# Attention layer, one core: one key bank of each row maximum read as a difference, with a relu on ScalarE

## The chip, the cores and the metric

The kernel runs on one core of one Trainium2 chip. The metric is the device time of one execution in microseconds, the median of several runs. The trace is of one profiled execution of its own.

## The reference

The input is x of shape (2, 4096, 256). It is layer-normalised to xn. The output is x + attention(xn) + experts(xn). The experts are eight small gated networks with routing weights. The attention has 16 heads of 16 columns, in two batches, so 32 heads in all:

```python
q, k, v = (xn @ W.T + b for each)            # reshaped to 16 heads of 16 columns
scores = einsum('bqhd,bkhd->bhqk', q * 16 ** -0.5, k)      # 4096 x 4096 per head
probs = softmax(scores)
out = einsum('bhqk,bkhd->bqhd', probs, v) @ Wo.T + bo
```

The kernel subtracts each row's maximum before the exponentials, so the maximum over the 4096 scores of a row is needed first.

## The kernel before

There are four phases. A setup phase splits the weights into a high and a low part. The token phase (16 groups of 512 tokens, g) computes the norm, the routing, the experts, and q, k and v. For q and k ScalarE writes the high part (L425) and VectorE the low part (L575), and SP stores both to `parts_d`. The attention phase follows, and an output phase ends the kernel.

The attention goes over 64 half heads (`s`): for each of 32 heads, first the queries 0 to 2047 and then 2048 to 4095. Two things run side by side for a half head.

- Scores of the half head `s` itself, transposed: keys on partitions, 512 queries as columns. `score` (L857) fills one of three banks `st`, ScalarE's exp (L951) reads it into a ring of 16 slots `pr`, and `times_v` (L865) multiplies by V, with a column of ones for the denominator, into `pv`. Four products for four groups of queries run in four column groups of the array. `values` issues them for the key block two behind.
- Maxima of the half head `s + 1`: `max_bank` (L844) computes 128 queries against 512 keys into one of four banks `sc`. A tile is 128 queries and eight such banks (`BANKS`). VectorE reduces the banks to six numbers per query (`MAXIMA`): banks 0 and 1 in one instruction, 2, 3, then 4 and 5 in one, 6, 7 (L971). The maxima run two tiles ahead (`AHEAD`).

The rows of q and k stand twice in SBUF: partitions 0 to 49 serve the scores, partitions 64 to 111 the maxima. So a score and a maxima matmul can run at the same time in two row groups of the array. In the loop over `r` (16 tiles per half head) TensorE issues for each of eight `i` one score and one maxima matmul; after i = 2 the products of one key block in whole width (512 columns), after i = 5 and i = 7 those of the next block in two halves of 256 columns.

Each engine has its own order of instructions, written out by hand, and semaphores between them: a score waits until the exp of three scores before has been read (`st_read`), a maxima matmul until the bank of four before has been reduced (`sc_read`), an exp waits for its score (`st_full`), a maximum for its banks (`sc_full`). When all maxima of a half head are there, VectorE turns them into two rows of the query operand in four small instructions (L976, L980, L984, L991). Once per half head ScalarE copies the sums `pv` to `oT` (`sums_kept`, L940), after the exps of key block 1 of the next half head; the products of key block 2 wait for it (`sums_ready`). Once per head VectorE inverts the denominators (L997).

The maxima of the first half head, and two tiles of the second, run before any score: first banks 0 to 3 of all 16 tiles, then banks 4 to 7 (`first_order`). In the last half head no maxima are left; the scores then use seven banks and alternate between the two row groups.

SP loads the rows of the next head from `parts_d` in 12 transfers (`head_rows`), spread over the head before; `qk_loaded` counts them.

Of the kernel before, what the change touches and what calls it, by code (L numbers as in the profile page):

```python
# [11 lines left out]
P = 128  # L12
# [34 lines left out]
TINY = 1e-8  # L47
DMA = 16
# [41 lines left out]

def first_head(nc, c, parts):

    for part_n in parts:
        w, half = ((0, 0), (1, 0), (1, 1), (0, 1))[part_n]
        for grp in range(2):
            for term in range(3):
                head_rows(nc, c, w, 0, 0, grp, term, half * QH, QH).then_inc(c.first_in[part_n], DMA)
# [116 lines left out]
def token_phase(nc, a, c):  # L214
    with ExitStack() as ctx:
# [3 lines left out]
        xn = sb("xn", [P, TPG, D], F32)  # L219
        xT = [[sb(f"xT{i}{hl}", [P, KC, GT], F32R) for hl in range(2)] for i in range(2)]  # L220
# [42 lines left out]
        vchain = sem("vector_chain")  # L263
        passed = sem("passed")
# [14 lines left out]
        def _(sp):  # L279
# [44 lines left out]
            sp.wait_ge(last_base_stored, DMA)  # L324
            for i in range(2):
# [74 lines left out]
        def _(act):  # L400
# [9 lines left out]
            def misc_unit(g, par, n):  # L410
# [12 lines left out]
                bias = c.bqs if kind == "q" else c.bk  # L423
                act.wait_ge(parts_stored[u % 2], (g * (SPLITS // 2) + u // 2 + 1) * DMA)
# [9 lines left out]
            def body(g, par, last, more):  # L434
                for e in range(E):
# [17 lines left out]
        def _(pool):  # L453
            def base_start(g, par):
# [4 lines left out]
                ins.then_inc(base_init, 1)  # L459

# [4 lines left out]
            def body(g, par, last, more):  # L465
                for e in range(E):
# [4 lines left out]
                    if e == 0 and not last:  # L471
                        base_start(g + 1, 1 - par)

# [5 lines left out]
        def _(dve):  # L479
# [78 lines left out]
            def misc_unit(g, par, n):  # L558
# [62 lines left out]
def attention_phase(nc, a, c):  # L621
# [3 lines left out]
    with ExitStack() as ctx:  # L625
# [4 lines left out]
        oT = sb("oT", [P, GT], F32)  # L630
        mx = [sb(f"mx{i}", [P, QT, MAXIMA], F32) for i in range(2)]
# [16 lines left out]
        sc_read = sem("sc_read")  # L648
        max_chain = sem("max_chain")
# [21 lines left out]
        QK_LOADS = 2 * 3 * 2  # L671
        V_LOADS = 4
# [26 lines left out]

        def reductions(g):  # L700

            return 3 * (g // RINGB) + (1, 1, 2, 3)[g % RINGB]
# [18 lines left out]
        def first_order(g):  # L721

            if g >= QT * BANKS:
                return divmod(g % (QT * BANKS), BANKS)
            half, rest = divmod(g, QT * RINGB)
            return rest // RINGB, half * RINGB + rest % RINGB

        @block.sync
        def _(sp):
            def load(n, par, piece):  # L730

                w, rest = divmod(QK_LOADS - 1 - piece, QK_LOADS // 2)
                grp, term = divmod(rest, 3)
                head_rows(nc, c, w, par, n, grp, term, 0, S).then_inc(qk_loaded, DMA)
# [103 lines left out]
        def _(pe):  # L838
            def max_bank(g, t, b, par, hf, grp):

                r0, q0 = 64 * grp, hf * QH + t * P
                if g >= RINGB:
                    pe.wait_ge(sc_read, reductions(g - RINGB))
# [27 lines left out]
            for g in range((QT + AHEAD) * BANKS):  # L871
                for part_n in WHEN_IN.get(g, ()):
                    pe.wait_ge(c.first_in[part_n], 2 * 3 * DMA)
                t, b = first_order(g)
                max_bank(g, t, b, 0, g // (QT * BANKS), g % 2)
            pe.wait_ge(c.ones_in, RING * 2 * DMA)

            def body(h0, heads, at):
                first, last = at == 0, at + heads == HEADS
                for q in range(2 * heads):  # L880
# [16 lines left out]
                    if here == SUPERS - 1:  # L897
                        for kb in range(KB):
                            for j in range(QSUB):
                                score(s, QSUB * kb + j, par, hf, here, j % 2)  # L900
                            values(kb, 0, GT)
                        continue
                    for r in range(KB // 2):
                        t = r + AHEAD
                        to = q + 1 + t // QT
                        if hf == 0 and t == QT and not (last and q // 2 == heads - 1):
                            pe.wait_ge(qk_loaded, (n + 1) * QK_LOADS * DMA)
                        for i in range(BANKS):
# [23 lines left out]
        def _(act):  # L932
# [32 lines left out]
        def _(dve):  # L965
            def maximum(g, t, i, par):

                c, col = divmod(i, 3)
                first, n = ((0, 2), (2, 1), (3, 1))[col]
                dve.wait_ge(sc_full, g + RINGB * c + first + n)  # L970
                nc.vector.reduce_max(mx[par][:, t, i:i + 1], sc_bank(first, n), AX.X).then_inc(sc_read, 1)  # L971
# [27 lines left out]
            for half in range(2):  # L999
                for t in range(QT):  # L1000
                    for i in range(3 * half, 3 * half + 3):
                        maximum((half * QT + t) * RINGB - half * RINGB, t, i, 0)
# [4 lines left out]
            for t in range(AHEAD):  # L1007
                for i in range(MAXIMA):
                    maximum((QT + t) * BANKS, t, i, 1)

            def body(h0, heads, at):
                first, last = at == 0, at + heads == HEADS
                for q in range(2 * heads):
                    s = 2 * h0 + q
                    for r in range(KB // 2):
                        t = r + AHEAD
                        to = s + 1 + t // QT
                        for i in range(MAXIMA):
                            if to < SUPERS:
                                maximum(((s + 1) * QT + t) * BANKS, t % QT, i, to % 2)  # L1020
# [124 lines left out]
def layer(nc, x, Wq, bq, Wk, bk, Wv, bv, Wo, bo, Wg, Wu, Wd, Wr, temperature, out):  # L1145
# [8 lines left out]
    c.base_d = nc.dram_tensor("base_d", (TOK, D), F32, kind="Internal").ap()  # L1154
    c.v_d = nc.dram_tensor("v_d", (TOK, D), F32, kind="Internal").ap()
# [40 lines left out]
```

## Time and profile before

| | |
|---|---|
| median of 3 runs | 6275.22 us (6273.61 to 6275.73) |
| profiled execution | 6268.36 us |
| its span, first to last instruction | 6266.6 us |
| TensorE busy | 6156.2 us (98%) |
| VectorE busy | 5532.0 us (88%) |
| ScalarE busy | 4840.4 us (77%) |
| GpSimd busy | 512.8 us (8%) |

The token phase ends at about 1300 us; the maxima run from 1316.0 to 6116.4 us. A busy share is an average over the stages. An instruction's duration runs from its start to the end of its writes; neighbours on one engine overlap, so the distance between two starts can be less than the duration.

### The profile page before, as it was taken

The numbers are of one execution on the slowest core, as the hardware profiler recorded it, in microseconds if no ns is written. First come the engines' busy times: TensorE is split into PE (matmuls) and PEld (weight loads), VectorE is DVE, ScalarE is ACT, GpSimd is POOL, SyncE is SP. The second block draws the span as 40 slices with busy tenths as digits, with TensorE's granted clock in tenths as the row PEclk, the third lists the DMA queues.
The fourth block names the chain that finished last, engine by engine and source line by source line (L and its number), as shares of the span: only waits on it lengthen the run. The fifth ranks groups of instructions, "written<-read, shape, count | busy, mean of one in ns | idle before, by whom it ended". The sixth has DMA issues, their size and how long they took to land. (4 is left out here: it accounts for less than half of the span.)

```text
span 6266.6 us, 120405 instructions
## 1 busy us (share of the span) xinstructions
PE 6156.2 (98%) x48392; PEld 3140.4 (50%) x48392; DVE 5532.0 (88%) x8291; ACT 4840.4 (77%) x9069; POOL 512.8 (8%) x535
## 2 busy tenths in 40 slices
PE   6999999989999999999999999999999999999998
PEld 5888888854444444444444444444444444444444
DVE  5555555579999999999999999999999999999993
ACT  3444333318898888888988888988889898988886
POOL 2333322210000000000000000000000000000000
PEclk9999999969999999999999999999999999999999
DMA  3111111111111121111111111111111111111113
GB/s 100 48 48 48 48 48 48 41 28 27 34 34 34 35 36 32 30 30 30 31 31 31 30 31 30 31 31 30 30 30 30 35 34 34 34 34 35 34 50 129
DMA packets 243304, 244.68 MB, mean 39 GB/s; under 512 B 159472, under 2 KB 204272, under 8 KB 236400
## 3 DMA queue, kind: packets, MB, share of 16 engines
q1 hardware_dynamic: 231720, 206.04, 15.0%
q0 software_dynamic: 11024, 30.94, 2.1%
q8 instruction: 379, 6.21, 0.4%
q14 instruction: 181, 1.48, 0.1%
HBM read 159.26 MB, written 76.58 MB: 38 GB/s over the span
## 5 line engine op out<-in xcount | busy, mean ns | idle before, releaser
L971 DVE TENSOR_REDUCE mx<-sc 128x1 f32<-128x512 f32 (+1 forms) x6144 | 4785.1, 856 | 9.4 <-PE sc L844 8.9
L951 ACT ACTIVATE pr<-st 128x512 f32<-128x512 f32 x8120 | 4268.0, 603 | 479.1 <-PE st L857 475.1
L844 PE MATMUL sc<-experts 48*128 48x512 f32 x8192 | 2824.6, 446 | 21.4 <-DVE mx L971 13.8
L857 PE MATMUL st<-experts 50*128 50x512 f32 x8120 | 2694.7, 431 | 0.1
L865 PE MATMUL pv<-pr,vst 128*32 128x256 f32 (+1 forms) x24440 | 2397.0, 464 | 2.0 <-ACT pr L951 0.9
L857 PEld LDWEIGHTS st<-experts 50*128 50x128 f32 x8120 | 1306.6, 184 | 1827.2 <-ACT pr L951 1654.6
L844 PEld LDWEIGHTS sc<-experts 48*128 48x128 f32 x8192 | 1328.5, 186 | 92.6 <-DVE mx L971 75.1
L865 PEld LDWEIGHTS pv<-pr,vst 128*32 128x32 f32 x24440 | 481.7, 108 | 955.3 <-issue 907.8
L438 ACT ACTIVATE gated<-gate 128x512 f32<-128x512 f32 x256 | 152.0, 597 | 567.3 <-PE up L75 567.0
L606 DVE TENSOR_TENSOR hraw<-gated,up 128x512 f32<-128x512 f32 x256 | 174.5, 686 | 416.4 <-ACT gated L438 404.2
L75 PE MATMUL down<-experts,hid 128*128 128x256 f32 x3072 | 390.2, 283 | 15.1 <-POOL hid L469 15.1
L469 POOL TENSOR_TENSOR hid<-hraw,hid 128x512 fp32r<-128x512 f32 x256 | 325.6, 1293 | 890.9 <-ACT hid L441 890.9
L75 PEld LDWEIGHTS down<-experts,hid 128*128 128x128 f32 x3072 | 384.2, 191 | 27.0 <-POOL hid L469 18.3
L75 PE MATMUL gate<-xT,experts 128*128 128x512 f32 x1536 | 392.9, 391 | 0.0
L75 PE MATMUL up<-xT,experts 128*128 128x512 f32 x1536 | 389.8, 389 | 0.0
L75 PEld LDWEIGHTS up<-xT,experts 128*128 128x128 f32 x1536 | 288.4, 188 | 60.2
L822 POOL DMA_DIRECT2D den<-den_d x32 | 17.3, 540 | 3626.9 <-DMA den_d<-oT 3626.9
L75 PEld LDWEIGHTS gate<-xT,experts 128*128 128x128 f32 x1536 | 283.2, 188 | 55.1
L587 DVE SCALAR_TENSOR_TENSOR base<-down,wts,base 128x256 f32<-128x256 f32 x512 | 222.6, 478 | 74.8 <-PE down L75 74.3
L441 ACT ACTIVATE hid<-hraw 128x512 fp32r<-128x512 f32 x256 | 160.5, 629 | 47.7 <-DVE hraw L606 47.7
L75 PE MATMUL misc<-xT,wT 128*128 128x512 f32 x384 | 95.7, 399 | 6.4 <-DVE part L575 6.4
L824 POOL DMA_DIRECT2D rden_d<-rden x32 | 17.2, 538 | 879.6 <-DVE rden L997 879.6
(105 smaller groups left out, 1280.9 us busy)
## 6 DMA issues: line engine op xcount, KB each, us to landing
experts<-parts_d SPq DMA_DIRECT2D x372, 256.0 KB, 4.3
parts_d<-part SPq DMA_DIRECT2D x64, 512.0 KB, 2.8
x_in<-in_L_attn_hidden_states SPq DMA_DIRECT2D x16, 512.0 KB, 4.6
v_d<-v_sb SPq DMA_DIRECT2D x32, 256.0 KB, 2.1
vst<-v_d SPq DMA_DIRECT2D x128, 64.0 KB, 2.2
sums_d<-oT SPq DMA_DIRECT2D x256, 32.0 KB
whole<-sums_d POOLq DMA_DIRECT2D x32, 256.0 KB, 3.0
recs<-rden_d POOLq DMA_DIRECT2D x32, 256.0 KB, 5.5
```

The lines of the kernel that those rows point to most:

```text
L75: last = nc.tensor.matmul(out, lhs[k][a], rhs[k][b], start=(n == 0), stop=(n == len(terms) - 1))
L438: nc.scalar.activation(gated[half][:, :], gate[half][:, :], ACT.Silu).then_inc(silu_done, 1)
L441: nc.scalar.activation(hid[e % 2][0][:, half, :], hraw[half][:, :], ACT.Identity).then_inc(hh_ready, 1)
L469: nc.gpsimd.tensor_tensor(hid[e % 2][1][:, half, :], hraw[half][:, :], hid[e % 2][0][:, half, :], ALU.subtract).then_inc(hl_ready, 1)
L587: ins = nc.vector.scalar_tensor_tensor(out=base[par][:, t, :], in0=down[hf][:, j, :], scalar=wts[par][:, t, e:e + 1], in1=base[par][:, t, ...
L606: nc.vector.tensor_tensor(hraw[half][:, :], gated[half][:, :], up[half][:, :], ALU.mult).then_inc(hid_ready, 1)
L822: nc.gpsimd.dma_start(den[:, :], c.den_d[bass.ds(n, 1), :].rearrange("o (p f) -> (o p) f", p=P)).then_inc(den_in, DMA)
L844: nc.tensor.matmul(sc_bank(g % RINGB), qr[par][r0:r0 + TERMS, q0:q0 + P], kr[par][r0:r0 + TERMS, b * GT:(b + 1) * GT], start=True, stop=Tr ...
L857: nc.tensor.matmul(score_bank(at, x), kr[par][r0:r0 + ROWSM, kb * P:(kb + 1) * P], qr[par][r0:r0 + ROWSM, q0:q0 + GT], start=True, stop=Tr ...
L865: last = nc.tensor.matmul(pv[VC * j:VC * (j + 1), c0:c1], vst[par][:, kb, :], pr[:, (QSUB * kb + j) % PRING, c0:c1], start=(kb == 0 and c0 ...
L951: nc.scalar.activation(pr[:, (QSUB * kb + j) % PRING, :], score_bank(2 * at + q, x), ACT.Exp).then_inc(st_read, 1)
L971: nc.vector.reduce_max(mx[par][:, t, i:i + 1], sc_bank(first, n), AX.X).then_inc(sc_read, 1)
```

## The change

The maximum of the last two key banks is rewritten. For a query, with s6 and s7 its scores against one key of group 6 and the key of group 7 at the same place, max(s6, s7) = s6 + relu(s7 - s6), and s7 - s6 is one matmul against the difference of the keys, k7 - k6. The token phase makes these key differences (`kd`, for two groups per batch), splits them into a high and a low part and stores them to `kd_d`. In the partitions that serve the maxima, the last 512 columns of k hold them in place of the last keys (`difference_rows`). Bank 6 of a tile is then filled from the difference, bank 7 from the keys of group 6. ScalarE reads bank 6 with a relu into `ahead` in SBUF (`above`, after the exp of x % 8 == 6), and VectorE does one `tensor_tensor_reduce` of bank 7 and `ahead`, add and then maximum. VectorE reduces a tile in six instructions as before, now banks 0 and 1 together, 2, 3, 4, 5, and 7 with `ahead`. The maxima matmul that refills bank 6 waits for the relu, not for VectorE.

The products with V are issued at other places of the tile, the first head's tiles follow the same scheme, and a head's rows come in 15 transfers. In the last four key blocks of the last half head the scores use only row group 0, since the other group no longer holds these keys.

```diff
+def difference_rows(nc, c, par, n, term):
+    r0 = 64 + HD * term
+    return nc.sync.dma_start(kept_rows(c, par)[1][r0:r0 + HD, S - GT:S].bitcast(F32), c.kd_d[ORDER[1][term], n * HD:(n + 1) * HD, :])
...
+                if kind == "k" and g % GPB == GPB - 2:
+                    if g >= GPB:
+                        act.wait_ge(kd_stored, g // GPB * KC * DMA)
+                    nc.scalar.activation(kd[:, 1, i, :].bitcast(F32), bank[:, :], ACT.Identity, bias=bias[:, i:i + 1]).then_inc(k_kept, 1)
...
+                        if e == E - 1 and (g + 1) % GPB == GPB - 1:
+                            for i in range(KC):
+                                act.wait_ge(k_apart, (g + 1) // GPB * KC + i + 1)
+                                nc.scalar.activation(kd[:, 0, i, :], kd[:, 1, i, :].bitcast(F32), ACT.Identity).then_inc(kd_high, 1)
...
+            def store_difference(b):
+                for i in range(KC):
+                    pool.wait_ge(kd_high, b * KC + i + 1)
+                    nc.gpsimd.tensor_tensor(kd[:, 1, i, :], kd[:, 1, i, :].bitcast(F32), kd[:, 0, i, :], ALU.subtract).then_inc(kd_low, 1)
+                for i in range(KC):
+                    pool.wait_ge(kd_low, b * KC + i + 1)
+                    pool.dma_start(c.kd_d[:, b * D + i * P:b * D + (i + 1) * P, :].rearrange("r p t -> p r t"),
+                                   kd[:, :, i, :].bitcast(F32)).then_inc(kd_stored, DMA)
...
+                    if kind == "k" and g % GPB == GPB - 1:
+                        dve.wait_ge(k_kept, g // GPB * KC + i + 1)
+                        nc.vector.scalar_tensor_tensor(out=kd[:, 1, i, :].bitcast(F32), in0=misc[(par * len(MISC) + n) % 2][:, :], scalar=bias[:, i:i + 1],
+                                                       in1=kd[:, 1, i, :].bitcast(F32), op0=ALU.add, op1=ALU.subtract).then_inc(k_apart, 1)
...
+        DIFFERENCE = BANKS - 2
+        KEYS_APART = tuple(range(DIFFERENCE)) + (BANKS - 1, DIFFERENCE)
...
-                if g >= RINGB:
-                    pe.wait_ge(sc_read, reductions(g - RINGB))
+                before = g - RINGB
+                if before >= 0:
+                    if placed(before)[1] == DIFFERENCE:
+                        pe.wait_ge(d_read, placed(before)[0] + 1)
+                    else:
+                        pe.wait_ge(sc_read, reductions(before))
+                b = KEYS_APART[b]
...
-                            if i == 2:
-                                values(2 * r, 0, GT)
-                            if i == 5:
-                                values(2 * r + 1, 0, GT // 2)
-                            if i == 7:
-                                values(2 * r + 1, GT // 2, GT)
+                            if i == 1:
+                                values(2 * r, 0, GT // 2)
+                            if i == 3:
+                                values(2 * r, GT // 2, GT)
+                            if i == 6:
+                                values(2 * r + 1, 0, GT)
...
+            def above(g):
+                if g >= SUPERS * QT * BANKS:
+                    return
+                tile = placed(g)[0]
+                act.wait_ge(sc_full, g + 1)
+                if tile >= 2:
+                    act.wait_ge(sc_read, reductions(last_bank(tile - 2)))
+                nc.scalar.activation(ahead[:, tile % 2, :], sc_bank(g % RINGB), ACT.Relu).then_inc(d_read, 1)
+            for t in range(QT + AHEAD):
+                above(last_bank(t) - 1)
...
+                            if x % BANKS == DIFFERENCE:
+                                above(((s + 1) * QT + kb // 2 + AHEAD) * BANKS + DIFFERENCE)
...
+            def maximum(g, tile, i):
+                first, n = ((0, 2), (2, 1), (3, 1), (4, 1), (5, 1), (7, 1))[i]
+                column = mx[tile // QT % 2][:, tile % QT, i:i + 1]
+                dve.wait_ge(sc_full, g + first + n)
+                if first < DIFFERENCE:
+                    nc.vector.reduce_max(column, sc_bank(first % RINGB, n), AX.X).then_inc(sc_read, 1)
+                    return
+                dve.wait_ge(d_read, tile + 1)
+                nc.vector.tensor_tensor_reduce(out=summed[:, :], in0=sc_bank(first % RINGB), in1=ahead[:, tile % 2, :], scale=1.0, scalar=LOWEST,
+                                               op0=ALU.add, op1=ALU.max, accum_out=column).then_inc(sc_read, 1)
```

## Rows read from the trace of the kernel before

**Rows 1.** The page, its first part: span, and busy us by engine.

```profile
span 6266.6 us, 120405 instructions
PE 6156.2 (98%) x48392; PEld 3140.4 (50%) x48392; DVE 5532.0 (88%) x8291; ACT 4840.4 (77%) x9069; POOL 512.8 (8%) x535
```

**Rows 2.** Busy time by stage: token, first maxima, steady stretch; columns in the first row.

```profile
core 0: us, PE busy (x) PEld busy (x) DVE busy (x) ACT busy (x) POOL busy (x), PEclk, DMA share, GB/s
200.00:1200.00 1000.00, 987.76 (x5742) 875.50 (x5741) 540.36 (x1427) 397.70 (x612) 299.91 (x258) 1.00 0.14 47
1316.00:1400.00 84.00, 70.17 (x145) 30.47 (x145) 83.86 (x111) 0.57 (x1) 0.00 (x0) 0.50 0.16 23
2500.00:3500.00 1000.00, 999.96 (x8538) 410.31 (x8534) 1000.00 (x1344) 898.61 (x1721) 25.58 (x38) 1.00 0.16 29
```

**Rows 3.** Groups by form, 2500 to 3500 us: busy, mean ns, idle before.

```profile
L951 ACT ACTIVATE pr<-st 128x512 f32<-128x512 f32 x1708 | 894.7, 598 | 101.4 <-PE st L857 100.6
```

**Rows 4.** Timeline of one tile: start us, length us, engine, line, instruction.

```profile
3000.50 1.57 ACT L951 ACTIVATE pr<-st 128x512 f32<-128x512 f32 x3 [0.21 <-PE st L857]
...
3000.80 1.06 PE L865 MATMUL pv<-pr,vst 128*32 128x512 f32 x8
...
3001.79 0.49 PE L857 MATMUL st<-experts 50*128 50x512 f32 x1
...
3002.10 0.18 PEld L844 LDWEIGHTS sc<-experts 48*128 48x128 f32 x1
...
3002.13 0.46 PE L844 MATMUL sc<-experts 48*128 48x512 f32 x1
...
3002.32 2.62 ACT L951 ACTIVATE pr<-st 128x512 f32<-128x512 f32 x5 [0.25 <-PE st L857]
...
3002.75 0.64 PE L865 MATMUL pv<-pr,vst 128*32 128x256 f32 x8
...
3003.32 0.50 PE L857 MATMUL st<-experts 50*128 50x512 f32 x1
...
3003.66 0.39 PE L857 MATMUL st<-experts 50*128 50x512 f32 x1
...
3004.55 0.50 PE L857 MATMUL st<-experts 50*128 50x512 f32 x1
```

**Rows 5.** Timeline of VectorE alone in the same tile, four of its instructions.

```profile
3000.84 1.21 DVE L971 TENSOR_REDUCE mx<-sc 128x1 f32<-128x1024 f32 x1
...
3002.57 0.67 DVE L971 TENSOR_REDUCE mx<-sc 128x1 f32<-128x512 f32 x1
3003.16 1.21 DVE L971 TENSOR_REDUCE mx<-sc 128x1 f32<-128x1024 f32 x1
3004.30 0.67 DVE L971 TENSOR_REDUCE mx<-sc 128x1 f32<-128x512 f32 x1
```

**Rows 6.** Timeline where a half head's sums are copied out.

```profile
3056.44 0.60 ACT L940 ACTIVATE oT<-pv 128x512 f32<-128x512 f32 x1
...
3056.91 1.60 ACT L951 ACTIVATE pr<-st 128x512 f32<-128x512 f32 x3
...
3057.14 1.06 PE L865 MATMUL pv<-pr,vst 128*32 128x512 f32 x8
```

**Rows 7.** Groups by form, 2500 to 3500 us: VectorE's small operations.

```profile
L976 DVE TENSOR_REDUCE nm<-mx 128x16 f32<-128x96 f32 x14 | 3.3, 237 | 0.0
...
L991 DVE STREAM_TRANSPOSE turned<-nmp 128x32 f32<-128x32 f32 x14 | 2.7, 196 | 0.0
L984 DVE TENSOR_TENSOR nmp<-nm,nmp 128x16 fp32r<-128x16 f32 x14 | 2.2, 159 | 0.0
L980 DVE CAST nmp<-nm 128x16 fp32r<-128x16 f32 x14 | 2.2, 158 | 0.0
L997 DVE RECIPROCAL rden<-den 128x32 f32<-128x32 f32 x6 | 2.0, 336 | 0.0
```

**Rows 8.** Chain of work that ended last: start us, length us, two adds.

```profile
6234.10 1.30 DVE o_base L1136 x2
```

More of the change, by code:

```diff
@@ L47 @@
 TINY = 1e-8
+LOWEST = -3.4028234663852886e38
 DMA = 16
@@ L96, in first_head @@
             for term in range(3):
-                head_rows(nc, c, w, 0, 0, grp, term, half * QH, QH).then_inc(c.first_in[part_n], DMA)
+                split = w and half and grp
+                head_rows(nc, c, w, 0, 0, grp, term, half * QH, QH - GT if split else QH).then_inc(c.first_in[part_n], DMA)
+                if split:
+                    difference_rows(nc, c, 0, 0, term).then_inc(c.first_in[part_n], DMA)
 def setup_phase(nc, a, c):
@@ L263, in token_phase @@
         vchain = sem("vector_chain")
+        k_kept = sem("second_last_keys_kept")
+        k_apart = sem("keys_subtracted")
+        kd_high = sem("difference_high_ready")
+        kd_low = sem("difference_low_ready")
+        kd_stored = sem("difference_stored")
         passed = sem("passed")
@@ L324, in _ @@
             sp.wait_ge(last_base_stored, DMA)
+            sp.wait_ge(kd_stored, B * KC * DMA)
             for i in range(2):
@@ L472, in body @@
                         base_start(g + 1, 1 - par)
+                    if e == E - 1 and (g + 1) % GPB == GPB - 1 and not last:
+                        store_difference((g + 1) // GPB)
             in_groups(before, body)
@@ L630, in attention_phase @@
         oT = sb("oT", [P, GT], F32)
+        ahead = sb("ahead", [P, 2, GT], F32)
+        summed = sb("summed", [P, GT], F32)
         mx = [sb(f"mx{i}", [P, QT, MAXIMA], F32) for i in range(2)]
@@ L648, in attention_phase @@
         sc_read = sem("sc_read")
+        d_read = sem("difference_read")
         max_chain = sem("max_chain")
@@ L671, in attention_phase @@
         QK_LOADS = 2 * 3 * 2
+        QK_MOVES = QK_LOADS + 3
         V_LOADS = 4
@@ L698, in sc_bank, with placed, last_bank @@
             return sc[:, i * GT:(i + n) * GT]
-        def reductions(g):
-            return 3 * (g // RINGB) + (1, 1, 2, 3)[g % RINGB]
+        COUNT = (1, 1, 2, 3, 4, 5, 5, 6)
+        def placed(g):
+            if g >= QT * BANKS:
+                return divmod(g, BANKS)
+            half, rest = divmod(g, QT * RINGB)
+            return rest // RINGB, half * RINGB + rest % RINGB
+        def reductions(g):
+            tile, i = placed(g)
+            if g >= QT * BANKS:
+                return MAXIMA * tile + COUNT[i]
+            return COUNT[3] * tile + COUNT[i] + (COUNT[3] * (QT - 1) if i >= RINGB else 0)
+        def last_bank(tile):
+            return QT * RINGB + RINGB * tile + RINGB - 1 if tile < QT else tile * BANKS + BANKS - 1
+        DIFFERENCE = BANKS - 2
+        KEYS_APART = tuple(range(DIFFERENCE)) + (BANKS - 1, DIFFERENCE)
         WHEN_IN = {0: (0, 1), QT * RINGB: (2,), QT * BANKS: (3,)}
@@ L719, in rows_of @@
             return dram[g * GT:(g + 1) * GT, :].rearrange("(t p) d -> p t d", p=P)
[L721 to L726, printed above, removed]
         @block.sync
@@ L733, in load @@
                 grp, term = divmod(rest, 3)
-                head_rows(nc, c, w, par, n, grp, term, 0, S).then_inc(qk_loaded, DMA)
+                split = w and grp
+                head_rows(nc, c, w, par, n, grp, term, 0, S - GT if split else S).then_inc(qk_loaded, DMA)
+                if split:
+                    difference_rows(nc, c, par, n, term).then_inc(qk_loaded, DMA)
             def load_v(n, par, piece):
@@ L872, in _ @@
                 for part_n in WHEN_IN.get(g, ()):
-                    pe.wait_ge(c.first_in[part_n], 2 * 3 * DMA)
-                t, b = first_order(g)
-                max_bank(g, t, b, 0, g // (QT * BANKS), g % 2)
+                    pe.wait_ge(c.first_in[part_n], (9 if part_n == 2 else 6) * DMA)
+                t, b = placed(g)
+                max_bank(g, t % QT, b, 0, g // (QT * BANKS), g % 2 if g < QT * RINGB else 1 - g % 2)
             pe.wait_ge(c.ones_in, RING * 2 * DMA)
@@ L899, in body @@
                             for j in range(QSUB):
-                                score(s, QSUB * kb + j, par, hf, here, j % 2)
+                                score(s, QSUB * kb + j, par, hf, here, j % 2 if kb < KB - GT // P else 0)
                             values(kb, 0, GT)
@@ L906, in body @@
                         if hf == 0 and t == QT and not (last and q // 2 == heads - 1):
-                            pe.wait_ge(qk_loaded, (n + 1) * QK_LOADS * DMA)
+                            pe.wait_ge(qk_loaded, (n + 1) * QK_MOVES * DMA)
                         for i in range(BANKS):
@@ L1001, in _ @@
                     for i in range(3 * half, 3 * half + 3):
-                        maximum((half * QT + t) * RINGB - half * RINGB, t, i, 0)
+                        maximum((half * QT + t) * RINGB - half * RINGB, t, i)
             negated(0, 0)
@@ L1008, in _ @@
                 for i in range(MAXIMA):
-                    maximum((QT + t) * BANKS, t, i, 1)
+                    maximum((QT + t) * BANKS, QT + t, i)
             def body(h0, heads, at):
@@ L1019, in body @@
                             if to < SUPERS:
-                                maximum(((s + 1) * QT + t) * BANKS, t % QT, i, to % 2)
+                                maximum(((s + 1) * QT + t) * BANKS, (s + 1) * QT + t, i)
                             if t == QT and s + 1 < SUPERS:
```

7 lines of the change are left out of this document (2 added, 5 removed).

## Prediction

> **What bounds the kernel now.** I read the page for the time of each engine, the windows for the stages, the groups of the steady stretch by form, and then the timeline of one tile. The profiled run took 6268.36 us for a span of 6266.6 [rows 1]; the median shown is 6275.22, so 7 us are added to my sum at the end. Four fifths of the span is the attention. There VectorE has no idle time (1000.00 of 1000 us), TensorE is busy for 999.96 and ScalarE for 898.6 [rows 2]. A busy TensorE says little, so I lay out a tile (128 queries against 4096 keys).
>
> VectorE: single-bank maxima start 0.60 us apart and a double takes 1.13 until the next start [rows 5]. Four singles and two doubles make 4 x 0.598 + 2 x 1.131 = 4.65 us. The trace gives eight exps in 8 x 1000 / 1708 = 4.68 us per tile [rows 3]. The rest of 0.03 are the small operations of the row maxima: 0.16, 0.08, 0.08 and 0.12 us per half head (their durations less the 0.08 by which neighbours overlap) and one reciprocal of 0.26 per head [rows 7], about 0.57 us per 16 tiles. So VectorE sets the pace.
>
> TensorE, if nobody held it: a group of two pairs (score and maxima matmul side by side) takes 0.66 from its first start to the products with V, one of three 0.89, each further pair 0.235; the products take 0.99 in whole width and 0.57 in half [rows 4] (3000.80 to 3001.79; 3002.75 to 3003.32). Sum 0.89 + 0.89 + 0.66 + 0.99 + 0.57 + 0.57 = 4.58. That is only 0.08 under the pace. ScalarE: three exps in 1.57 us, the first 0.60 long, so 0.49 each in a chain; eight are 3.9.
>
> **The change, part by part.** (1) VectorE loses one bank of eight: before, the second double and two singles (1.13 + 1.20) took banks 4 to 7; now two singles (1.20) and one add-and-maximum. The trace has no such operation. The nearest rows are an add of a PSUM and an SBUF operand, two in 1.30, 0.61 each in a row [rows 8], and small operations that cost 0.08 in a row [rows 7]. From below it is 0.60 (the maximum as an operation of one pass); from above 0.80, if the reduced value is fetched in an operation of its own that costs a full 0.20, the duration of the transpose of 32 columns [rows 7]. I take 0.60 + 0.07 = 0.67, near the small ones. VectorE's own work is then 1.13 + 4 x 0.60 + 0.67 = 4.19 per tile: no longer a bound by itself, and not what decides.
>
> The Trainium skill, "VectorE: DVE Perf Modes", section "Two Vector instructions with no wait between them", says that an operation that also writes out its accumulator is two instructions, the main one and an accumulator read. No row here shows it; it has no figure for the second, and it speaks for the upper half of the bounds.
>
> (2) ScalarE gets a relu per tile between exps 6 and 7, and the add-and-maximum waits for it. The same form in the same chain (oT, between exps) costs 0.47 to the next start [rows 6], so 0.49: nine are 4.41, plus 0.49 of oT per 16 tiles, 4.44 per tile. Not a bound by sum, but ScalarE now has hardly any slack, and the score ring has three banks. What counts is the loop of waits. From rows 4: a score's result comes 0.49 after the group starts; exp begins 0.04 later (3001.79 + 0.49 to 3002.32) and lasts 0.60. A bank whose reader ends is filled 0.55 later (double ended 3000.84 + 1.21 = 3002.05 [rows 5], load 3002.10, matmul ends 3002.59). Products with V start 0.07 before the last result ends (3003.66 + 0.39 against 3004.55 - 0.57).
>
> *Loop A*, one tile: score 4 is first of its group: 0.49 + 0.04 + 0.60 = 1.13 until exp 4 ends; exps 5, 6, relu, exps 7 and 0: 5 x 0.49 = 2.45; score 3 needs exp 0's bank: 0.55; then -0.07 + 0.57 of products until score 4 starts: 0.50. Sum 4.63. Without the relu it is 4.14, which is why it does not show now.
>
> *Loop B*, two tiles: exp 4 ends 1.13, relu ends 3 x 0.49 = 1.47 later; add-and-maximum 0.04 + 0.67 + 0.08; the next tile's double 1.13, then bank 2's maximum 0.60, whose release lets bank 6 be filled, 0.55; -0.07 + 0.99 of whole-width products; then TensorE alone to score 4: 0.89 + 0.57 + 0.66 + 0.57 = 2.69. Sum 9.28, half of it 4.64. So both loops leave 4.64 where 4.654 was: the bank saved yields 0.014 per tile, 0.2 us per half head.
>
> (3) The products with V are moved: half width after pair 1, half after pair 3, whole after pair 6. The floor stays 4.58. But the first ones of a half head's third block wait until ScalarE has copied the accumulator out (oT). Now that copy ends at 3057.04 and the products start at 3057.14 instead of about 3057.06: met almost exactly [rows 6]. After the change, counted from score 4 of the tile before: exps end at 1.13, e7 behind the relu 4 x 0.49 later, the copy 0.49 later: 3.58, plus 0.09 until products start: 3.67. TensorE would be there at 0.89 + 0.99 + 0.89 = 2.78, or 2.9 with loop B's delay. So this wait, with exps 0 to 2 queued behind the copy and all of TensorE behind the products, costs 0.8 us per half head. VectorE's small operations (0.16 + 0.08 + 0.08 + 0.12 = 0.44, and 0.13 for half a reciprocal) lie in loop B. All could cost 1.4; the loops absorb a little of one another, I take 1.3.
>
> Sum per half head (16 tiles): before 16 x 4.654 + 0.57 = 75.03; after 16 x 4.64 + 1.3 = 75.54. That is +0.5, times 63 half heads with maxima running beside them: +32 us.
>
> (4) The first head: 18 tiles run before ScalarE has exps, and VectorE is busy 83.86 of 84 us although TensorE's clock is at 0.50, its 1.2 GHz level [rows 2]. Banks 4 to 7 cost 2.33 now and 1.20 + 0.67 = 1.87 then: -0.46 x 18 = -8 us. The relu runs on an idle engine.
>
> (5) Token stage: for two key groups of 16, two more ScalarE copies of 0.6 us, two VectorE passes of 0.7 and, once a batch, two ScalarE copies, two GpSimd subtractions of about 1.3 and two stores. TensorE is busy 988 of 1000 us there, the others 540, 398 and 300 [rows 2]: hidden, +1. If that cover failed: under 4 us per batch. SP issues 15 loads per head instead of 12, same bytes, at 0.16 DMA share [rows 2], with the wait for them far off: 0.
>
> (6) The last half head: in its last four key blocks the scores lose the alternation of row groups. Four in one group take 1.13 and the products 0.99 against ScalarE's 4 x 0.49 = 1.96: at most 4 x 0.16. +0.5.
>
> Total 32 - 8 + 1.5 = +25: 6268.4 + 25 = 6293 for the profiled execution, 6300 beside the median of 6275.2.
>
> **Rivals.** A change under 0.2% (12.5 us) can't be told from none.
> *TensorE becomes the bound (faster).* The loops rest on latencies of a few hundredths. If a filled bank follows its release by 0.45 and not by 0.55, both loops fall to or under the floor of 4.58, and only the wait for oT stays: 16 x 4.58 + 0.85 = 74.13, -0.9 x 63 - 8 = -65: 6210. For it speaks that VectorE has half a microsecond per tile to give; against it that 0.55 is read from a real wait. It wins once the loops are under 4.62. Chance 0.22.
> *Gain and loss cancel.* The add-and-maximum at 0.60 and the loops at A's 4.63: 16 x 4.63 + 1.1 = 75.2, +9 - 9: 6275. Chance 0.15 of within 0.2% with its neighbours.
> *The add-and-maximum is dear.* At 0.80 loop B is 4.70: 16 x 4.70 + 1.3 = 76.5, +1.5 x 63 = +93, first head -6: 6362. At 1.0, 4.80: 6460. Chance 0.15.
> *ScalarE's chain is slower with the relu.* If each of the five links of loop A cost 0.03 more (0.11 more is the upper bound, an exp's whole 0.60 without overlap), the loop would be 4.63 + 0.15 = 4.78: 16 x 4.78 + 1.0 = 77.5, +2.5 x 63 - 8 = +150: 6425. Rows of this form speak against it: 0.49 in the chain of three [rows 4], 0.47 between starts around oT [rows 6]. Chance 0.03.
> The Trainium skill, "ScalarE: Activation LUTs", section "What ACT_TABLE_LOAD costs", gives an ACTIVATE with immediate scale and bias 186 ns + 0.833 N, less 93 ns overlap back to back: an estimate of 0.52 us for 512 columns. That is about this rival's link. The trace has 0.49, and by the trace I go.
> *My forecast*, loops at 4.63 to 4.67: chance 0.45.
>
> **Numbers.** 6300, itself 6285 to 6330. The range takes in most of the faster case and the dear operation: 6215 to 6370. Faster 0.23, same 0.16, slower 0.61.
>
> **What would show it.** VectorE idle for about 0.4 us per tile, put down to ScalarE's relu; ScalarE at 94 to 95% busy; the relu in chains of 0.49; half heads of 75.5 us; a TensorE stall of 0.8 us on oT once per half head; first maxima stage 8 us shorter; next start after an add-and-maximum 0.67 later. The forecast is wrong if VectorE idles and half heads are under 74.8 (latencies shorter than laid out, or the copy of oT hidden), or if that operation takes over 0.75.

## The result, and the profile after

The changed kernel takes 6362.53 us, median of 4 runs (6361.88 to 6364.21), against 6275.4 for the kernel before. The ratio is 1.0141, with a 95% interval from 1.0127 to 1.0155: 87 us slower. The forecast was 6300 and slower: 25 us more, where 87 were measured.

The page of the changed kernel, its first part:

```profile
span 6360.1 us, 124618 instructions
...
PE 6205.0 (98%) x48392; PEld 3169.6 (50%) x48392; DVE 5104.6 (80%) x9319; ACT 5214.5 (82%) x10101; POOL 520.0 (8%) x543
```

Beside [rows 1]: VectorE (DVE) has lost 427 us of work, ScalarE (ACT) has gained 374, and the span has grown by 93.5. The stages tell where. The windows of the changed kernel; columns as in [rows 2]:

```profile
200.00:1200.00 1000.00, 987.77 (x5743) 875.47 (x5742) 543.36 (x1430) 401.09 (x618) 303.59 (x262) 1.00 0.14 48
1316.00:1400.00 84.00, 74.48 (x174) 34.25 (x176) 80.74 (x138) 17.59 (x30) 1.05 (x4) 0.50 0.19 24
2500.00:3500.00 1000.00, 990.53 (x8360) 407.31 (x8352) 891.19 (x1523) 954.75 (x1895) 27.48 (x41) 1.00 0.17 31
```

In the steady stretch VectorE now idles for 109 of 1000 us, and no other engine is full in its place: ScalarE 955, TensorE 991 instead of 999.96. If no engine is full, something else must set the pace; the forecast said that it would be a loop of waits.

The first start of the maxima and of the scores, from the list of instructions on the tiles `sc` and `st`; before, then after. The length of the first maxima stage is the distance between the two first starts:

```profile
L844 PE MATMUL sc<-experts x8192: 383/447/793, 1315.1 to 6115.2; 48*128 48x512 f32 x200
...
L857 PE MATMUL st<-experts x8120: 383/394/794, 1398.6 to 6185.7; 50*128 50x512 f32 x199
```
```profile
L908 PE MATMUL sc<-experts x8192: 383/491/794, 1316.6 to 6206.9; 48*128 48x512 f32 x200
...
L921 PE MATMUL st<-experts x8120: 383/394/792, 1392.1 to 6277.9; 50*128 50x512 f32 x199
```

The token stage ends 1.5 us later. The first maxima stage takes 75.5 us instead of 83.5: 8 less. For the half heads I use the copies of the sums, one per half head. Before, then after; min/median/max ns, first and last start:

```profile
L940 ACT ACTIVATE oT<-pv x64: 597/605/685, 1482.0 to 6190.3; 128x512 f32<-128x512 f32 x64
```
```profile
L1004 ACT ACTIVATE oT<-pv x64: 592/594/637, 1475.7 to 6281.8; 128x512 f32<-128x512 f32 x64
```

The copy before the last one starts at 6221.2 after the change and at 6129.6 before it: the last half head, without maxima, takes 60.6 and 60.7. The 62 others take (6281.8 - 1475.7 - 60.6) / 62 = 76.54 us each, where they took (6190.3 - 1482.0 - 60.7) / 62 = 74.96. That is +1.58 a half head, +98 us over 62. With +1.5, -8 and +2 in the tail it makes the 93.5 of the spans. So the whole loss is in the steady half heads. I call this number "half head" below.

The groups of the steady stretch, 2500 to 3500 us of the changed kernel, by form:

```profile
L1028 ACT ACTIVATE pr<-st 128x512 f32<-128x512 f32 x1673 | 871.4, 610 | 45.3 <-PE st L921 43.6
...
L1054 DVE CUSTOM_DVE_ANT_0 summed<-sc,ahead 128x512 f32<-128x512 f32 x210 | 145.2, 691 | 106.5 <-PE sc L908 90.7 <-ACT ahead L1014 15.1
L1014 ACT ACTIVATE ahead<-sc 128x512 f32<-128x512 f32 x209 | 129.2, 618 | 0.0
...
L1054 DVE DVE_READ_ACCUMULATOR2_ANT mx<- 128x1 f32 x209 | 17.3, 83 | 0.0
```

Nearly all of VectorE's idle time stands before the add-and-maximum: 106.5 of 109 us, for 210 of them. The accumulator read is an instruction of its own, of 83 ns. What it costs is in the timeline of one tile of the changed kernel:

```profile
3001.06 0.62 ACT L1014 ACTIVATE ahead<-sc 128x512 f32<-128x512 f32 x1
...
3001.54 2.59 ACT L1028 ACTIVATE pr<-st 128x512 f32<-128x512 f32 x5
...
3001.82 0.69 DVE L1054 CUSTOM_DVE_ANT_0 summed<-sc,ahead 128x512 f32<-128x512 f32 x1 [0.81 <-ACT ahead L1014]
...
3002.44 0.08 DVE L1054 DVE_READ_ACCUMULATOR2_ANT mx<- 128x1 f32 x1
3002.44 3.61 DVE L1051 TENSOR_REDUCE mx<-sc 128x1 f32<-128x1024 f32 x5
...
3003.71 0.49 PE L921 MATMUL st<-experts 50*128 50x512 f32 x1
...
3004.30 1.57 ACT L1028 ACTIVATE pr<-st 128x512 f32<-128x512 f32 x3 [0.17 <-PE st L921]
...
3005.75 0.62 ACT L1014 ACTIVATE ahead<-sc 128x512 f32<-128x512 f32 x1
```

The next maximum starts with the accumulator read, 0.62 after the add-and-maximum: the read is free. From relu to relu the tile takes 4.69 us, not 4.64. And here is the missing piece: score 4 starts at 3003.71 and ends at 3004.20; exp 4 starts at 3004.30. That is 0.10 later, and so it is in 205 of the 209 tiles of this stretch. The 0.04 of the forecast came from exp 3 [rows 4], which waits only for its score. Exp 4 is the first of a key block and waits also for a free slot of `pr`. That wait had long been met: the products that free the slot ran from 2999.92 to 3000.98. The trace before had this too, at exp 0, two rows that I did not use:

```profile
2999.90 0.50 PE L857 MATMUL st<-experts 50*128 50x512 f32 x1
...
3000.50 1.57 ACT L951 ACTIVATE pr<-st 128x512 f32<-128x512 f32 x3 [0.21 <-PE st L857]
```

The add-and-maximum too waits for two things (bank 7 and the relu): the relu ends at 3001.06 + 0.62 = 3001.68, it starts at 3001.82, 0.14 later. The profile books most of this wait (90.7 us) to bank 7's matmul and 15.1 us to the relu. But the start stands 0.14 behind the relu's end in 207 of the 209 tiles, and at changing distances behind the matmul, so it is the relu that releases it. With these two values loop A is 4.63 + 0.06 = 4.69, and loop B (9.28 - 0.05 + 0.06 + 0.10) / 2 = 4.69 or 4.70. Both are equal to the tile that the trace shows.

Once per half head the copy of the sums stops TensorE:

```profile
3006.75 0.60 ACT L1004 ACTIVATE oT<-pv 128x512 f32<-128x512 f32 x1
...
3007.40 0.64 PE L929 MATMUL pv<-pr,vst 128*32 128x256 f32 x8 [0.71 <-ACT oT L1004]
```

The copy ends at 3007.35 and the products start at 3007.40. The third score of their group had started at 3006.29. In the tile before, such products started 0.33 us behind the third score's start, so these could have started at 3006.62. The stall is 0.78 us.

### The profile page after: what moved, and what is told of

Its sections match the earlier page's. It is cut to its first block and busy times, and to the rows that moved or that the text cites. A ratio compares the mean times of both kernels' runs of the same rounds, so it can differ in the third digit from the quotient of the medians.

```text
span 6360.1 us, 124618 instructions
## 1 busy us (share of the span) xinstructions
PE 6205.0 (98%) x48392; PEld 3169.6 (50%) x48392; DVE 5104.6 (80%) x9319; ACT 5214.5 (82%) x10101; POOL 520.0 (8%) x543
## 5 line engine op out<-in xcount | busy, mean ns | idle before, releaser
L1051 DVE TENSOR_REDUCE mx<-sc 128x1 f32<-128x512 f32 (+1 forms) x5120 | 3719.2, 787 | 24.0 <-PE sc L908 24.0
L908 PE MATMUL sc<-experts 48*128 48x512 f32 x8192 | 2877.8, 451 | 17.4 <-PEq L225 9.4
L921 PEld LDWEIGHTS st<-experts 50*128 50x128 f32 x8120 | 1335.6, 184 | 1942.0 <-ACT pr L1028 1819.5
L908 PEld LDWEIGHTS sc<-experts 48*128 48x128 f32 x8192 | 1352.2, 186 | 73.8 <-DVE mx L1051 40.2
L1054 DVE CUSTOM_DVE_ANT_0 summed<-sc,ahead 128x512 f32<-128x512 f32 x1024 | 707.9, 691 | 510.3 <-PE sc L908 441.3
L1014 ACT ACTIVATE ahead<-sc 128x512 f32<-128x512 f32 x1024 | 632.8, 618 | 79.3 <-PE sc L908 79.3
L76 PE MATMUL down<-experts,hid 128*128 128x256 f32 x3072 | 390.1, 283 | 15.1 <-POOL hid L504 15.1
```

What stands on the lines that cost most here:

```text
L76: last = nc.tensor.matmul(out, lhs[k][a], rhs[k][b], start=(n == 0), stop=(n == len(terms) - 1))
L908: nc.tensor.matmul(sc_bank(g % RINGB), qr[par][r0:r0 + TERMS, q0:q0 + P], kr[par][r0:r0 + TERMS, b * GT:(b + 1) * GT], start=True, stop=Tr ...
L921: nc.tensor.matmul(score_bank(at, x), kr[par][r0:r0 + ROWSM, kb * P:(kb + 1) * P], qr[par][r0:r0 + ROWSM, q0:q0 + GT], start=True, stop=Tr ...
L1014: nc.scalar.activation(ahead[:, tile % 2, :], sc_bank(g % RINGB), ACT.Relu).then_inc(d_read, 1)
L1051: nc.vector.reduce_max(column, sc_bank(first % RINGB, n), AX.X).then_inc(sc_read, 1)
L1054: nc.vector.tensor_tensor_reduce(out=summed[:, :], in0=sc_bank(first % RINGB), in1=ahead[:, tile % 2, :], scale=1.0, scalar=LOWEST, op0=AL ...
```

## The experiments

All ran against the kernel before. The half heads are from the first and last start of the oT copies of each run, as above (last half head 60.6 to 61.1).

| run | median us | ratio (95% interval) | half head us |
|---|---|---|---|
| before | 6273 to 6275 | | 74.96 |
| after | 6362.53 | 1.0141 (1.0127 to 1.0155) | 76.54 |
| e1 wait off exp 4 | 6329.94 | 1.0089 (1.0074 to 1.0104) | 76.01 |
| e2 copy of sums earlier | 6341.67 | 1.0107 (1.0090 to 1.0124) | 76.20 |
| e3 no relu | 6236.14 | 0.9938 (0.9923 to 0.9953) | 74.50 |
| e4 before, products moved | 6312.83 | 1.0061 (1.0046 to 1.0076) | 75.58 |
| e5 relu that nobody waits for | 6267.39 | 0.9990 (0.9981 to 1.0000) | 75.02 |
| e6 e1 and e2 | 6306.51 | 1.0052 (1.0037 to 1.0067) | 75.63 |
| e7 products at the old places | 6647.18 | 1.0594 (1.0578 to 1.0610) | 81.02 |
| e8 relu after exp 2 | 6278.28 | 1.0007 (0.9998 to 1.0016) | 75.21 |
| e9 e8 with the double on banks 0, 1 | 6286.19 | 1.0022 (1.0014 to 1.0031) | 75.35 |
| e10 e8 with the wait off exp 0 | 6225.46 | 0.9924 (0.9910 to 0.9937) | 74.33 |

### e1: the slot wait moved off exp 4

```diff
-                        act.wait_ge(pv_done, s * KB + kb + 1)
+                        if 2 * at + q == SUPERS - 1:
+                            act.wait_ge(pv_done, s * KB + kb + 1)
+                        elif kb % 2 == 0:
+                            act.wait_ge(pv_done, s * KB + kb + 2)
```

> The changed kernel with one wait moved: the wait of exp for a free slot of pr (pv_done) stands ahead of exp 0 of each tile for both key blocks, no longer ahead of exp 4. Theory 1 (loop A sets the pace, and its missing 0.06 us is that exp 4, which waits for two things, starts 0.10 after its score and not 0.04): a tile falls from 4.70 to 4.64 or 4.65, a half head from 76.5 to 75.7, the time from 6362 to 6310 to 6325. Theory 2 (loop B, through the add-and-maximum, sets the pace by itself): its exp 4 link is shorter too, but half as much per tile: 76.1 per half head, 6335 to 6345. Theory 3 (ScalarE or a port is slower for another reason): no change, 6362.

It took 6329.94 us, 33 less than the changed kernel. Exp 4 now starts right behind its score (3104.25 + 0.50 to 3104.78), and the relus, one per tile, stand like this:

```profile
3104.25 0.50 PE L921 MATMUL st<-experts 50*128 50x512 f32 x1
```
```profile
3104.78 0.60 ACT L1031 ACTIVATE pr<-st 128x512 f32<-128x512 f32 x1
...
3101.52 0.62 ACT L1014 ACTIVATE ahead<-sc 128x512 f32<-128x512 f32 x1
...
3106.23 0.62 ACT L1014 ACTIVATE ahead<-sc 128x512 f32<-128x512 f32 x1
...
3110.86 0.62 ACT L1014 ACTIVATE ahead<-sc 128x512 f32<-128x512 f32 x1
```

These tiles alternate, 4.71 and 4.63. 4.63 is loop A without the 0.06. The pair takes 9.34, 4.67 a tile, which is what a loop over two tiles does: loop B is left, (9.28 - 0.05 + 0.10) / 2 = 4.665. Not every tile alternates: from 3012 to 3058 us they take 4.65 to 4.69, which is the same over two. The time lies between theories 1 and 2, and the half head, 76.01, next to the 76.1 of theory 2: the double wait costs what was said, and behind it the second loop stands 0.04 lower.

### e2: the copy of the sums before exp 7

```diff
-                        if kb == 1 and not (first and q == 0):
-                            sums_kept(s - 1)
...
+                            if kb == 1 and j == DIFFERENCE - QSUB and not (first and q == 0):
+                                sums_kept(s - 1)
```

> The changed kernel with the copy of the sums (oT) between the relu and exp 7 of the half head's first tile, one link earlier. Theory 1 (the products of key block 2 stand still 0.8 us per half head because the copy sits behind the relu and exp 7): the stall falls from 0.8 to 0.3, part of it comes back because exp 7 is 0.49 later; 0.3 to 0.4 us less per half head, 6338 to 6345. Theory 2 (the copy waits for the last products of the half head before, not for ScalarE's order): nothing changes, 6362.

It took 6341.67 us, 21 less; a half head lost 0.34. In the list of waits, 2500 to 3500 us, the products stood for 5.0 us on 7 copies in the changed kernel and for 1.5 in this one. The waits at the six other copies of the stretch are in a row of their own, without a releaser: 4.5 us and 1.6.

```profile
PE pv L929 <- ACT oT L1004: 5.0, 7, 0.7
PE pv L929 <- issue: 4.5, 6, 0.8
```
```profile
PE pv L929 <- issue: 1.6, 6, 0.3
PE pv L929 <- ACT oT L1004: 1.5, 7, 0.2
```

The stall comes from the place of the copy in ScalarE's order.

### e3: no relu

After the first 18 tiles this kernel leaves the relu out. The add-and-maximum reads a tile of zeros (`nothing`) instead, so the maximum leaves out the keys of group 7, and the matmul that refills bank 6 waits for nothing. The core of the edit:

```diff
-                            if x % BANKS == DIFFERENCE:
-                                above(((s + 1) * QT + kb // 2 + AHEAD) * BANKS + DIFFERENCE)
...
-                        pe.wait_ge(d_read, placed(before)[0] + 1)
+                        if placed(before)[0] < QT + AHEAD:
+                            pe.wait_ge(d_read, placed(before)[0] + 1)
...
-                dve.wait_ge(d_read, tile + 1)
+                dve.wait_ge(d_read, min(tile, QT + AHEAD - 1) + 1)
...
-                nc.vector.tensor_tensor_reduce(out=summed[:, :], in0=sc_bank(first % RINGB), in1=ahead[:, tile % 2, :], scale=1.0, scalar=LOWEST,
+                nc.vector.tensor_tensor_reduce(out=summed[:, :], in0=sc_bank(first % RINGB), in1=ahead[:, tile % 2, :] if tile < QT + AHEAD else nothing[:, :], scale=1.0, scalar=LOWEST,
```

> The changed kernel without the relu after the first 18 tiles: the add-and-maximum reads a constant tile of zeros, so bank 6 counts for nothing in the maximum. Theory 1 (the relu's link in ScalarE's chain sets the pace): loop A falls to 4.20, and TensorE alone is left with 4.58 a tile; half head 74.4, the time 6225 to 6235, under the kernel before. Theory 2 (the add-and-maximum or its accumulator read costs the time): half head stays near 76.5, 6350 to 6362. Theory 3 (TensorE's own work has grown by the moved products): half head 75 or more, 6270 and over.

It took 6236.14 us, 126 less than the changed kernel and less than the kernel before. The add-and-maximum, its accumulator read and the moved products are all still there, and so is the stall on the copy. Most tiles take 4.58 to 4.60. The half head is 74.50 = 16 x 4.58 + 1.2: TensorE's floor and what stops it. So it is the relu and what waits for it that cost the time, and VectorE's relief was real.

### e4: the kernel before with the products moved

```diff
-                            if i == 2:
-                                values(2 * r, 0, GT)
-                            if i == 5:
-                                values(2 * r + 1, 0, GT // 2)
-                            if i == 7:
-                                values(2 * r + 1, GT // 2, GT)
+                            if i == 1:
+                                values(2 * r, 0, GT // 2)
+                            if i == 3:
+                                values(2 * r, GT // 2, GT)
+                            if i == 6:
+                                values(2 * r + 1, 0, GT)
```

> The kernel before with the products with V at the changed places alone (half after pair 1, half after pair 3, whole after pair 6). Theory 1 (the new places bring the wait for oT forward): VectorE keeps 4.654 a tile, the copy of oT costs a stall of 0.3 to 0.6 us per half head; half head 75.5, the time 6300 to 6315. Theory 2 (the new places are free): 6275. The changed kernel loses 1.55 us per half head in all, so this also says how much of it is the order alone.

It took 6312.83 us, 39 more than the kernel before, in the expected span. A half head is 0.62 longer, and the list of waits, 2500 to 3500 us, has the row that the kernel before does not have:

```profile
PE pv L865 <- ACT oT L940: 4.5, 7, 0.7
```

So on the kernel before the new order alone costs 0.6 us per half head, by way of that wait; the changed kernel, which has the same wait, loses 1.58 in all.

### e5: a relu that nobody waits for

The kernel of e1, with the two VectorE edits of e3 (the wait for `d_read` and the constant operand). ScalarE's chain and TensorE's wait for bank 6 are those of e1. As in e3, the maximum leaves out the keys of group 7.

> The kernel of e1 (wait moved off exp 4), relu kept in ScalarE's chain after the first 18 tiles, but the add-and-maximum reads a constant tile of zeros and doesn't wait for it (bank 6 counts for nothing in the maximum). Theory 1 (in e1 loop B, the way relu - add-and-maximum - next double - bank 2 - bank 6, sets the pace at 4.67): without VectorE's wait only loop A is left with 4.63; the alternation of long and short tiles of e1 goes, a half head falls from 76.0 to 75.3 to 75.5, the time 6285 to 6300. Theory 2 (the relu's link in ScalarE's chain is all, loop B never counted): as e1, 6330.

It took 6267.39 us, 63 less than e1. Its relus:

```profile
3103.87 0.62 ACT L1016 ACTIVATE ahead<-sc 128x512 f32<-128x512 f32 x1
...
3108.50 0.62 ACT L1016 ACTIVATE ahead<-sc 128x512 f32<-128x512 f32 x1
...
3113.13 0.62 ACT L1016 ACTIVATE ahead<-sc 128x512 f32<-128x512 f32 x1
```

The alternation is gone, every tile is 4.63: loop A alone. This shows both loops apart: A has VectorE nowhere in it, B goes through the add-and-maximum. The half head fell by 1.0, more than the 0.5 to 0.7 expected. 16 x 0.04 = 0.64 is the tile. The other 0.35 I put down to VectorE's small operations, which lie in loop B; no run takes them apart.

### e6: e1 and e2 together

> e1 and e2 together: the wait off exp 4 and the copy of the sums before exp 7. Theory 1 (a loop per tile and a stall per half head, independent): the gains add, 32 + 21: a half head 75.6 to 75.7, 6305 to 6312. Rival (both shorten the same stall): 6325 to 6330.

It took 6306.51 us. A half head is 76.54 - 75.63 = 0.91 shorter, and the parts are 0.53 and 0.34: they add.

### e7: the products at the old places

The reverse of the edit of e4, on the changed kernel.

> The changed kernel with the products with V at the places of before (whole after pair 2, halves after pairs 5 and 7). Theory 1 (the loops run through TensorE's order): whole-width products after pair 2 and the late bank releases lie in one loop; laid out the same way a tile is about 5.05, half head 80 to 82, the time 6600 to 6700. Rival (the places matter only through the wait for oT, as in e4, where they cost 0.6 us per half head): 6325.

It took 6647.18 us, with a half head of 81.02 = 16 x 5.06. The relu between exps 6 and 7 does not go with the old places at all; the move of the products, which costs 0.6 by itself, saves 4.5 here. No run takes the loop with the 5.06 apart, but the trace lays it out:

```profile
3097.94 0.50 PE L921 MATMUL st<-experts 50*128 50x512 f32 x1 [0.19 <-ACT pr L1028]
...
3098.37 1.07 PE L929 MATMUL pv<-pr,vst 128*32 128x512 f32 x8
...
3099.36 0.50 PE L921 MATMUL st<-experts 50*128 50x512 f32 x1
...
3099.90 2.06 ACT L1028 ACTIVATE pr<-st 128x512 f32<-128x512 f32 x4 [0.54 <-PE st L921]
```

Score 2 waits for its bank: it starts 0.05 after exp 7 has ended, in 198 of 198 tiles of the stretch. Then come the whole-width products 0.43 later, score 3 0.99 after them, and exp 3 0.54 after that. From exp 3 to the end of exp 7, with the relu between, it is 3.05. The sum is 5.06: a loop over one tile, with the relu in it and VectorE nowhere.

### e8 and e9: the relu where ScalarE waits anyway

In the kernel before, ScalarE idles after exp 2, while TensorE does the whole-width products ([rows 4]: the chain of three from 3000.50 ends at 3002.07, the next exp starts at 3002.32). From the 17th tile on, e8 puts the difference into bank 2, the relu after exp 2, and the products back to their old places. The core of the edit:

```diff
-        DIFFERENCE = BANKS - 2
-        KEYS_APART = tuple(range(DIFFERENCE)) + (BANKS - 1, DIFFERENCE)
+        DIFFERENCE = 2
+        KEYS_APART = ((0, 1, 2, 3, 4, 5, 7, 6), (0, 1, 7, 2, 3, 4, 5, 6))
...
+        REDUCED = (((0, 2), (2, 1), (3, 1), (4, 1), (5, 1), (7, 1)),
+                   ((0, 1), (1, 1), (3, 1), (4, 2), (6, 1), (7, 1)))
```

e9 has ((0, 2), (3, 1), (4, 1), (5, 1), (6, 1), (7, 1)) for the second row.

> The change with the difference bank at another place, from the 17th tile on: the difference is bank 2 of a tile and not bank 6, its relu follows exp 2, the key group added to it is still bank 7; VectorE reduces 0, 1, 3, (4 and 5 together), 6, and 7 with ahead; the products with V are at the places of before. Theory 1 (the price of the relu is its place: between exps 6 and 7 it is a link of both loops, after exp 2 it falls into the time in which ScalarE waits for the score behind the whole-width products, and it ends long before bank 7 is there): a tile takes 4.63, a half head 74.4 to 74.6, the time 6231 to 6247, under the kernel before. Theory 2 (a ninth operation in ScalarE's chain costs the same wherever it stands): 6300 or more.

> As e8, but the double reduction of VectorE stays on banks 0 and 1, as in the change, and 4 and 5 are reduced one by one. Theory 1: a tile 4.63 as in e8, but VectorE's small operations of a half head now hold up bank 4 behind the double: 0.27 more per half head, 74.6 to 74.8, the time 6248 to 6262. Theory 2 (the place of the relu is all): as e8.

They took 6278.28 and 6286.19 us. Theory 2 of e8 is out: the same nine operations take 84 us less than in the changed kernel. Against e7, which has the products at the same places, it is 369 less. The relu, the difference bank and VectorE's grouping of the banks moved together, and no run moves the relu alone. The e8 kernel and the one before can't be told apart, 0.9998 to 1.0016. e9's half head is 0.14 longer than e8's, where 0.27 was expected. But the numbers of theory 1 were missed by 31 and 24 us. The rows of e8 say why:

```profile
3103.95 0.50 PE L927 MATMUL st<-experts 50*128 50x512 f32 x1
```
```profile
3104.55 0.60 ACT L1034 ACTIVATE pr<-st 128x512 f32<-128x512 f32 x1 [0.17 <-PE st L927]
```

In this order it is exp 0 that waits for its score, and exp 0 too is the first of a key block: score ends 3104.45, exp starts 3104.55, 0.10 again. The tile is 4.68 (relus at 3101.31 and 3105.99).

### e10: e8 with the wait moved ahead of exp 4

```diff
-                        act.wait_ge(pv_done, s * KB + kb + 1)
+                        if 2 * at + q == SUPERS - 1:
+                            act.wait_ge(pv_done, s * KB + kb + 1)
+                        elif kb % 2:
+                            act.wait_ge(pv_done, s * KB + kb + 2)
```

> e8 with the wait for a free slot of pr moved ahead of exp 4 for two key blocks, off exp 0, which in e8 is the exp that waits for its score. Theory 1 (an exp that has to wait twice starts 0.10 after its score's end and not 0.04, and in e8 this stands in the loop of a tile): the tile falls from 4.69 to 4.63, a half head from 75.2 to 74.3, the time from 6278 to 6218 to 6228, under the kernel before. Theory 2 (in e8 the pace is set by something else, the banks of the maxima): as e8.

It took 6225.46 us, 0.9924 of the kernel before (0.9910 to 0.9937): 49 us faster than before and 137 faster than the changed kernel. Its score 0 starts at 3104.16 and ends at 3104.66, exp 0 starts at 3104.69:

```profile
3104.16 0.50 PE L927 MATMUL st<-experts 50*128 50x512 f32 x1
```
```profile
3104.69 0.60 ACT L1037 ACTIVATE pr<-st 128x512 f32<-128x512 f32 x1
```

and in 2500 to 3500 us TensorE is busy again for 999.73 of 1000, ScalarE for 977:

```profile
2500.00:3500.00 1000.00, 999.73 (x8610) 392.23 (x8606) 916.56 (x1569) 976.92 (x1952) 24.56 (x37) 1.00 0.17 31
```

A half head is 74.33, 0.63 under the kernel before. The tile is 4.63, still above TensorE's 4.58. No run takes its loop apart, but by the trace one like loop A fits, begun at exp 0: 0.53 from score 0 to exp 0, 3.05 to the end of exp 4, 0.12 until score 7, and 0.93 until the next score 0 make 4.63. The same wait was not moved in the kernel before, whose exp 0 starts 0.10 behind its score too, so part of e10's gain could be open to that kernel as well. VectorE has no idle time there, which speaks against it. In the list of waits for the products on oT, 2.1 us for 7 copies are left, on the weight loads alone.

## Why the prediction was right, and where it was not

**Direction and mechanism: right.** The bank saved brings nothing, since two loops of waits through ScalarE's chain and through the add-and-maximum take the place of VectorE. e1 and e5 show them apart, and e3 shows TensorE's floor of 4.58 (the terms laid out for it add up to 4.57). VectorE idles 0.5 us a tile, where 0.4 was said, and ScalarE is at 95%, as said.

**Size: too small, and the range held by luck.** The loss was forecast at 25 us and is 87. The forecast's own mechanism was given 6285 to 6330, and 6362.53 is outside it. The wide range, 6215 to 6370, holds it because its upper end was there for a dear add-and-maximum. That rival gave 6362, the time measured, by a cost that the trace refutes.

**Part 2, "exp begins 0.04 later": the term that was mis-sized.** It holds for an exp with one wait. For exp 4, with two, it is 0.10 (e1, and e8 against e10 for exp 0). The tile was 4.70 and not 4.64. That is 16 x 0.06 = 1.0 us per half head and about 60 of the 62 us by which 6300 was too low. Exp 4's wait is not all of it: with that wait moved, 33 us came back (e1), because loop B, which had a late start of its own, then set the pace. The row with the 0.10 was in the trace.

**Loop B.** The add-and-maximum starts 0.14 after the relu's end, not 0.04, and takes 0.62 to the next start, not 0.67. Over two tiles the errors leave +0.05: 4.665 where 4.64 was said, without the term above.

**Part 1, the add-and-maximum.** 0.62, near the lower bound of 0.60. The accumulator read is an instruction of its own, as the Trainium skill says ("VectorE: DVE Perf Modes", section "Two Vector instructions with no wait between them"), and the trace agrees: 83 ns, but it starts together with the next maximum and moves nothing.

**ScalarE's link.** 0.49, as taken: from exp 4 (3004.30) to the copy behind exp 7 (3006.75) there are five links, the relu's among them, in 2.45 us. The 0.52 worked out from the Trainium skill ("ScalarE: Activation LUTs", section "What ACT_TABLE_LOAD costs") does not hold here.

**Part 3, the products.** The stall on oT was forecast at 0.8 and is 0.78; e4 prices the order at 0.62 per half head on the kernel before, e2 gets 0.34 of it back. With VectorE's small operations 1.3 were taken; 76.54 - 16 x 4.70 = 1.34 is left. The share of the small operations in it was not measured.

**Parts 4 to 6.** First maxima stage -8.0 (forecast -8), token stage +1.5 (+1). The last half head has not grown (60.6), 0.5 were taken.

**The faster rival** asked for loops under 4.62. They never were in this order of work; e5, which opens loop B, comes to 4.63.

## What to carry to other kernels

When the engine at the bound is relieved, add up the loops of waits, not only the work of each engine: work moved to an engine with 10% idle time in its stage was a loss, because it stood as a link in the chain that everyone waits for. Put such an operation where its engine waits anyway: the same relu after exp 2 instead of exp 6, with its bank, the products and one wait moved to suit it, turned +1.4% into -0.8%. Read start latencies from the very instruction that closes the loop. Where it waits for two semaphores, move the wait that is always met long before to an instruction that is not waited for.

## What the runs showed of the hardware

- An exp that waits for its score starts 0.04 us after the matmul's end with one wait, and 0.10 with two, although the second had long been met. It is 0.10 for exp 4 of the changed kernel in 205 of 209 tiles and 0.04 in e1 in all 211; 0.10 for exp 0 of e8 in 199 of 200 that waited and 0.04 in e10 in all 202. The second wait was the one for a slot of `pr` each time; no other was tried. In loops of this kind 0.06 us was worth 33 us of 6362 (e1) and 53 us of 6278 (e10).
- The fused add-and-maximum with its accumulator output (128 x 512, one operand in PSUM) takes 0.62 us from start to start, as much as a plain add [rows 8], and its accumulator read of 83 ns starts together with the next instruction. With its two waits it starts 0.14 us behind the relu that releases it, in 207 of 209 tiles.
- A copy of PSUM or a relu in a chain of exps takes 0.48 to 0.52 us until the next start, about as an exp does (0.48 to 0.49), and no table load shows between them, 2500 to 3500 us.
